# The product of the diagonals reads the identity from PSUM and stands ahead of the unit's sum

## The reference

```python
    scores, idx = jax.lax.top_k(sim, PK_TOPK)           
    ...
    final_scores, pk_idx = jax.lax.top_k(score, FINAL_TOPK)
    ...
    k = jnp.einsum('bnhk,bnhkd->bnhd', kv_scores, keys_table[ind])
    v = jnp.einsum('bnhk,bnhkd->bnhd', kv_scores, values_table[ind])
    sim = jnp.einsum('bihd,bjhd->bhij', q, k)
    ...
    out = jnp.einsum('bhij,bjhd->bhid', attn, v)
    ...
    return out @ Wo
x = x + _L0_gnn_ref(_layernorm(x, axis=-1), adj, L0_gnn_W, L0_gnn_a)
x = x + _L0_ffn_ref(_layernorm(x, axis=-1), ...)
```

## Time and profile before

| | before |
|---|---|
| median of 3 runs | 10248.68 us (10248.1 to 10253.65) |
| the profiled execution's own time | 10249.67 us |
| span of its profile | 10247.8 us |
| VectorE busy | 7529.4 us, 73% |
| GpSimd busy | 7738.2 us, 76% |
| TensorE busy | 5613.9 us, 55% |
| ScalarE busy | 1935.1 us, 19% |
| granted TensorE clock | 0.738 of full speed |

### The profile page before, as it was taken

How to read it: one execution, slowest core, us unless ns; L and a number is a source line. 1 busy time by engine, 2 the same in 40 slices (tenths; PEclk the granted TensorE clock), 3 DMA queues, 4 the chain that set the end, 5 groups by cost and what they waited for, 6 DMA issues and landing times.

```text
span 10247.8 us, 204962 instructions
## 1 busy us (share of the span) xinstructions
PE 5613.9 (55%) x23108; PEld 4466.6 (44%) x23108; DVE 7529.4 (73%) x43420; ACT 1935.1 (19%) x5738; POOL 7738.2 (76%) x7894
## 2 busy tenths in 40 slices
PE   4665555555555555555555555655555555555554
PEld 3444444444444444444444444444444444444443
DVE  8887777777777777777777777777777777766764
ACT  3211121111211112111121111211112111111111
POOL 5677777777777777777777777777777777777776
PEclk7777777777777777777777777777777777777777
DMA  3333333333333333333333333333333333333333
GB/s 109 98 108 107 107 112 108 107 107 106 112 108 107 108 107 111 108 108 107 107 111 107 106 107 109 110 107 107 108 109 110 107 107 107 108 109 107 108 108 97
DMA packets 525905, 1101.48 MB, mean 107 GB/s; under 512 B 213120, under 2 KB 271104, under 8 KB 524320
## 3 DMA queue, kind: packets, MB, share of 16 engines
q0 software_dynamic: 378096, 1032.96, 35.1%
q1 hardware_dynamic: 83248, 37.82, 1.5%
q10 hardware_dynamic: 63104, 18.63, 0.9%
HBM read 1084.36 MB, written 4.19 MB: 106 GB/s over the span
## 4 chain that ended last, share of the span: by engine, by line
POOL 71%; issue 23%; DVE 2%; ACTq 2%; PE 1%; DMA 0%; POOLq 0%; ACT 0%; SPq 0%; DVEq 0%
POOL ring L366 71%; ACTq L501 1%; DVE hot L1029 0%; ACTq L496 0%; DMA wo<-in_Wo 0%; DVE ps_v L943 0%; DMA far_row<-far_at 0%; PE ps_o L734 0%; POOLq L382 0%; POOLq L380 0%; DVE edge L872 0%; ACT L417 0%; PE ps_s L703 0%; DVE edge L885 0%; DVE row L876 0%
## 5 line engine op out<-in xcount | busy, mean ns | idle before, releaser
L366 POOL DMA_INDIRECT ring<-in_table,idx x7877 | 7736.6, 982 | 2484.9 <-issue 2402.4
L678 PE MATMUL ps_w<-ring,diag 128*128 128x256 f32 x8192 | 2037.3, 406 | 32.7 <-DMA ring<-in_table,idx 31.7
L690 PE MATMUL ps_t<-ident,kv 128*128 128x128 f32 x448 | 204.0, 455 | 2885.0 <-DVE kv L954 2885.0
L678 PEld LDWEIGHTS ps_w<-ring,diag 128*128 128x128 f32 x8192 | 1654.6, 207 | 284.6 <-issue 31.8
L940 DVE TENSOR_SCALAR ps_v<-ring,wgt 128x256 f32<-128x256 f32 x512 | 248.7, 486 | 1934.4 <-DMA ring<-in_table,idx 1931.4
L1029 DVE SCALAR_TENSOR_TENSOR hot<-rank,posf,cand 128x54 f32<-128x54 f32 x8192 | 1651.1, 267 | 0.3
L943 DVE SCALAR_TENSOR_TENSOR ps_v<-ring,wgt,ps_v 128x256 f32<-128x256 f32 x3072 | 1475.5, 480 | 19.7
L690 PEld LDWEIGHTS ps_t<-ident,kv 128*128 128x128 f32 x448 | 79.2, 177 | 2992.8 <-DVE kv L954 2992.8
L734 PEld LDWEIGHTS ps_o<-probT,kv 128*128 128x128 f32 x4480 | 992.4, 316 | 202.1 <-ACT probT L467 127.4
L734 PE MATMUL ps_o<-probT,kv 128*128 128x128 f32 x4480 | 988.2, 402 | 102.2 <-ACT probT L467 102.0
L722 PE MATMUL ps_p<-ident,prob 128*128 128x128 f32 x2304 | 422.5, 320 | 880.2 <-ACT prob L459 879.5
(11 more groups left out here) (125 smaller groups left out, 8120.4 us busy)
## 6 DMA issues: line engine op xcount, KB each, us to landing
far<-in_table SPq DMA_DIRECT2D x22304, 1.0 KB
far<-in_table ACTq DMA_DIRECT2D x18016, 1.0 KB
ring<-in_table,idx POOLq DMA_INDIRECT x7877
xin<-in_x SPq DMA_DIRECT2D x8, 512.0 KB
mask<-in_adj SPq DMA_DIRECT2D x1, 4096.0 KB, 14.3
out_x<-acc SPq DMA_DIRECT2D x64, 64.0 KB
far_row<-far_at ACTq DMA_DIRECT2D x188, 0.5 KB
far_row<-far_at SPq DMA_DIRECT2D x127, 0.5 KB
```

Source lines behind the costliest of these rows:

```text
L366: pool.indirect_dma_start(out=ring[:, t % RING, k, :], out_offset=None, in_=table, in_offset=bass.IndirectOffsetOnAxis(ap=idx[:, t, k:k + ...
L678: ins = nc.tensor.matmul(pw_ps, diag[:, k, :], ring[:, t % RING, k, :], start=(k == 0), stop=(k == PE_ROWS - 1))
L690: nc.tensor.transpose(ps_t[:, 0, :], made(t)[:, 0:P], ident[:]).then_inc(k_tp, 1)
```

## The change

The quarter of the bank `ps_w` from column 384 on gets a copy of the identity, made once by VectorE at the start (128x128 elements), after the projection and after a wait for ACT's two copies out of `wh_ps`. The product at L963 reads the identity from there instead of from SBUF. In `head` the product stands ahead of `sum_rows` instead of behind it, in both branches. (With the old order TensorE's graph sum in tile 3, which is released by `rows_summed`, could write into the bank while the product reads from it.) In the start (L1071, L1077) the order is as it was.

```diff
         ps_part = ps_v[:, 1, :]
+        ident_ps = ps_w[:, 3 * P:4 * P]
         oT_ps = ps_o[:, 0, :]
...
                 dve.wait_ge(pw_mm, n * UNITS + t)
                 dve.wait_ge(wgt_ready, n * UNITS + t + 1)
-                nc.vector.tensor_tensor(diag[:], ident[:].unsqueeze(1).broadcast_to([P, PE_ROWS, P]),
+                nc.vector.tensor_tensor(diag[:], ident_ps.unsqueeze(1).broadcast_to([P, PE_ROWS, P]),
                                         wgt[:, t, 0:PE_ROWS].unsqueeze(2).broadcast_to([P, PE_ROWS, P]),
                                         ALU.mult).then_inc(diag_ready, 1)
...
             projection(0)
+            dve.wait_ge(aux_copied, 2)
+            step(nc.vector.tensor_scalar(ident_ps, ident[:], 1.0, None, ALU.mult))
             dve.wait_ge(adj_dma, 16)
...
                         c = choose_sums(n, t, a_unit, c, add_row)
+                        diagonals(n if t < UNITS - 1 else n + 1, (t + 1) % UNITS)
                         sum_rows(n, t)
-                        diagonals(n if t < UNITS - 1 else n + 1, (t + 1) % UNITS)
                         choose_rows(t, a_unit, c)
                     else:
...
                             add_row(n, t, k)
-                        sum_rows(n, t)
                         if t < UNITS - 1:
                             diagonals(n, t + 1)
+                        sum_rows(n, t)
```

## The result

The changed kernel takes **10008.78 us** (median of 4 runs, 9999.84 to 10012.57); the kernel before, with its runs from the same comparison, 10251.17 us (10248.1 to 10263.26). The ratio is 0.976 (95% interval 0.9743 to 0.9777). The forecast was 10028 us, range 10004 to 10055. The profiled execution took 9999.84 us, the fastest of the four, and lies under that range; the median is 4.8 us inside it.

What follows compares the result with a forecast made beforehand. GpSimd's gathers were taken to bound the kernel: 10249.67 - 225.5 (hold gone) + 1.1 (start) + 4 (choice of rows) = 10029, or 10028 us against the median; range 10004 to 10055.

Steps and rivals of the forecast that it cites:

- The bound: GpSimd's gathers at L366: from 285.4 to 10222.8 us, time is their count times their period; GpSimd stays the bound.
- the rule of the hold: A gather whose point 0.13 us after its start meets a VectorE operation with two SBUF inputs waits for its end.
- (a): Product reading the identity from PSUM: still 1220 ns, no longer holds gathers; takes off 225.5 us, bounds 0 and 264.
- (b): Product ahead of the sum: sums come 1.13 us later, covered by VectorE's 4.4 us wait for rows a unit.
- Rival 3: VectorE becomes the bound in some units through late sums, needing over 2.8 us a unit: 10140 us, chance 0.05.
- (c): One copy of the identity to PSUM at the start, ahead of VectorE's mask wait: nothing, at most 0.4 us.
- The start: GpSimd's one wait at L381, near 285 us, for a sum now behind a product: +1.1 us on the path.
- (d): Choice of rows at L1029, 16 operations with two SBUF inputs, meets more gathers: +4 us, bounds -20 to +25.
- the graph's edges: Shorter two-SBUF-input operations that, with the choice of rows, make the other 39 us of gather stretch.
- Random phases: Gather phases against the 504 products look random; geometry then gives 220 us of stretch, beside the counted 225.5.

Runs made afterwards that it cites:

- e1: Kernel before with the identity from PSUM, product still behind the sum except in tile 3 of each head: 10001.68 us, ratio 0.9762.
- e4: Changed kernel with the product made twice, first with the identity from SBUF, then from PSUM: 10247.76 us, ratio 1.0002 to the kernel before.
- e5: Changed kernel with the product made twice, both times with the identity from PSUM: 10014.49 us, ratio 0.9772 to the kernel before.
- e0: Kernel before, unchanged, profiled again: median 10246.37 us, ratio 1.0004; the profiled execution took 10235.15 us.
- e9: Changed kernel, unchanged, run again on a third chip: 10025.89 us, ratio 0.9764 to the kernel before.
- e10: Identity from PSUM, product behind the sum except in tile 3, run again on a third chip: 10025.54 us, ratio 0.9764 to the kernel before.
- e8: Kernel before plus an unused maximum over 640 SBUF elements between sum and product, identity from SBUF: 10155.28 us, ratio 0.9911.
- e2: Changed kernel's order, product ahead of the sum, but identity still read from SBUF: 10223.89 us, ratio 0.9979 to the kernel before.

## Why the prediction was right

**The bound and the rule of the hold** hold in every run. The term of 225.5 us (a) came in whole: no gather is stretched beside the product. With the whole row counted it should have been 228.5. L1093 had told it rightly from the kernel before: an operation with one input in PSUM and one in SBUF holds nothing. The product's duration, taken as unchanged, is 1217 ns. The Trainium skill, SBUF — State Buffer, section Who interferes with whom, says that with two SBUF inputs the second comes through the read interface shared with GpSimd, and that with at most one, outside the 2-port modes, VectorE doesn't contend: e1, e4 and e5 agree with 0, 220.1 and 0 us beside the product. Its inference that a tensor_tensor doesn't hold up GpSimd's descriptor making can't be carried over to these gathers, as the 229.4 us before and e4 show; which part of a gather it is that waits, its descriptors or its reading of the indices, no run shows.

**Cover (b)** held: later sums moved waits about (238.3 to 431.4 us at the output row), and VectorE still had 1516.5 us of waiting for rows. Rival 3 needed this to run out; e5 took 600 us more of it and, past the start, cost nothing.

**The copy (c)** cost nothing: VectorE's wait for the mask is still there behind it, 6.4 us.

**The start** was put at +1.1 us. The steady run began 2.9 us later than in the first trace of before, 1.3 later than in e0. In e9 and e10, which differ in just this order, it began 0.1 us apart; and one kernel varies as much from run to run (285.6 and 287.2 for the kernel before, 286.7 and 288.5 for e1's). So the term is not refuted and not shown. What was named to tell it by, a wait of GpSimd longer by 1.1 us, failed: the wait grew by 6.0 us, since GpSimd came 3.1 us sooner.

**The step that failed in sign is (d)**, the choice of rows. I had the count right: 1292 points fell into the choice's operations in the changed kernel, 2.6 for each of 504 units, after 1092 (2.2) before. But I priced each as before. Those of before were not average. A product that holds a gather, as some 420 of the 504 do, fixes the phase of what follows: the first gather after it met the choice 1.25 us on and was stretched by 3.6 ns on average (500 points), the second, 2.5 us on, by 36.5 ns (500 points). Free of that lock the mean is 10.9 ns instead of 18.6, in all 14.1 us instead of 20.4. So -6 us stood in place of +4. The size is less sure than the sign: with one and the same count for all runs, the first pair has 21.7 and 15.5 us in the choice, e0 has 18.3, and the four other runs that hold nothing beside the product (e1, e5, e9, e10) have 16.4 to 17.0.

**What the sum missed.** Forecast: 10249.67 - 225.5 + 1.1 + 4 = 10029; the profiled execution took 9999.84. Of the 29 us, 13 are the undisturbed gather's 1.7 ns, which e0 shows to be the chip's or the run's; 10 are (d); 5 are the graph's edges, whose stretch the sum took as unchanged and which fell from 20.8 to 15.6 us (e0: 19.8); 3 are the points that the count of the product left out; and the start took 2 back.

The 13 us are the chance of one pair of profiles; most of the rest comes back in the other pairs. Medians on one chip fell by 242.4 us, 239.2 (e1) and 240.3 (e9) where the sum has 220, so some 20 us came back each time. The stretch says the same: all gathers together were 276.0 us longer than undisturbed ones before, 274.4 in e0, and 34.8 in the changed kernel. The sum took 225.5 off this and put 4 on; taken off were about 240.

**The range** was said to take (d)'s bounds, -20 and +25, around a forecast that has +4 in it. That gives 10004 and 10049; for 10055 there is no term. The median lies 4.8 us above the lower bound. That bound stood for phases that lock between the choice's reads; what brought the time near it was the end of a lock, the edges and the unlike profiles, so that it still fell inside is partly luck. The gathers' mean, forecast near 953 ns, is 950 for the same reasons.

**Random phases** gave 220 us, and the count gave 225.5; the agreement was partly luck. e8 and e2 show that the same product can cost 137.7 or 205.7 us by where it starts. It did no harm here because the sum took the counted 225.5, and because the change removes the hold at any phase; a sum for a change that only moves the product would have failed on it.

## What to carry to other kernels

When GpSimd issues gathers without a break and another engine seems to be beside the path, list the gathers by length, not only by mean: a median of 948 with a maximum of 1994 ns says that somebody holds them, and the end of the stretched ones minus the usual tail names the operation. Where phases are spread evenly, a VectorE operation with two SBUF inputs costs such gathers about the square of its length less 0.17 us over twice their period, each time (here 0.44 us for 1.22; e8's 137.7 us in 504 make 0.27). Give it one input from PSUM, or, nearly as good here, cut it into short ones, even though VectorE then does more. In such a sum, ask too what the other two-input operations will cost once the gathers aren't locked any more. Before a few microseconds of such a kernel are put down to a change, profile both kernels on one chip, and expect phases to lock.

## What the runs showed of the hardware that was not expected

- The length of an undisturbed indirect gather of 128 rows differs by chip or run: means of 947.1 ns in the first profile, 945.4 to 946.0 in nine others, 948.2 and 948.3 on a third chip. With 7877 of them that is up to 23 us, more than several terms of the sum.
- The hold has sharp edges. A gather's point in the first 0.16 us of a product's row costs nothing (58 gathers, at most 3 ns); anywhere later it costs the time to the product's end (428 gathers, within 0.014 us).
- A held gather fixes the phase of what follows. Of the choice's 16 short operations the cost hangs on the phase: 3.6 ns at 1.25 us behind the held gather, 36.5 ns at 2.5 us; without the lock, 10.9 on average.
- Idle-looking work can make a kernel faster: 416.1 us of a useless maximum took 89 us off the time, because the product behind it met fewer gathers.
